# A two-layer gated cross-attention and expert kernel: earlier ranks and scatters in layer one, a later weighing step in the linear experts, phases joined by one barrier

## The reference

```
x = x + tanh(g_xattn[0]) * attention0(layernorm(x), ctx)      # 16 heads, causal
x = x + tanh(g_ffn[0])   * (experts0(h) + shared0(h))         # h = layernorm(x)
x = x + tanh(g_xattn[1]) * attention1(layernorm(x), ctx)      # 16 heads, masked by a length
x = x + tanh(g_ffn[1])   * experts1(layernorm(x))
```

## Time and profile before

| | before |
|---|---|
| median of 3 runs | 1680.35 us (1679.78 to 1683.46) |
| the profiled execution: its time, its span | 1675.68 us, 1674.0 us |
| TensorE busy, granted clock over the span | 1395.6 us, 0.927 |
| VectorE, ScalarE, GpSimd busy | 1056.6, 799.0, 729.8 us |
| layer 0 from 60 to 531 us, linear experts 535 to 748 us | |
| layer 1 from 753 to 1236 us, its experts 1244 to 1674 us | |

### The profile page before, as it was taken

The page is one execution under the profiler, slowest core; times in us unless marked ns, Lnnn a source line. Parts: engine busy times, 40 slices in busy tenths (PEclk is TensorE's granted clock), DMA queues, the critical chain, the costliest instruction groups (busy, mean ns, idle before and its releaser), DMA issues. The chain is left out here.

```text
span 1674.0 us, 39790 instructions
## 1 busy us (share of the span) xinstructions
PE 1395.6 (83%) x12001; PEld 1168.8 (70%) x12002; DVE 1056.6 (63%) x3525; ACT 799.0 (48%) x1760; POOL 729.8 (44%) x710
## 2 busy tenths in 40 slices
PE   4898998989884777746899989988629999999997
PEld 3677777767663677744565666656419999999997
DVE  3677676866765454534788888887545545555543
ACT  2454554545441555542556555565404444444443
POOL 4234443444433466555245455553323524545422
PEclk9799898999996899886899999999959999999999
DMA  5634633342314577656445534433152433343422
GB/s 119 94 91 115 177 101 111 89 116 60 97 50 130 124 122 133 103 88 109 85 111 161 119 110 121 115 88 109 44 157 41 99 63 78 88 100 89 100 38 43
DMA packets 212268, 166.92 MB, mean 100 GB/s; under 512 B 21382, under 2 KB 205736, under 8 KB 211880
## 3 DMA queue, kind: packets, MB, share of 16 engines
q1 hardware_dynamic: 178472, 125.26, 29.0%
q0 software_dynamic: 26880, 35.80, 12.4%
q10 hardware_dynamic: 6784, 4.21, 1.5%
HBM read 63.80 MB, written 50.24 MB: 68 GB/s over the span
## 5 line engine op out<-in xcount | busy, mean ns | idle before, releaser
L1896 POOL DMA_INDIRECT out_rows<-e_y,e_token x68 | 109.8, 1615 | 236.2 <-DVE e_y L1952 216.4
L1978 ACT ACTIVATE e_h<-e_h,t_up_bias 128x256 f32<-128x256 f32 x272 | 110.5, 444 | 208.0 <-PE e_h L2014 208.0
L1316 ACT ACTIVATE a_probs<-a_scores_t 128x384 f32<-128x384 f32 (+1 forms) x256 | 138.0, 544 | 118.7 <-PE a_scores_t L1683 57.8
L969 DVE TENSOR_REDUCE a_row_max<-a_scores 128x2 f32<-128x512 f32 x256 | 168.7, 677 | 19.3 <-PE a_scores L1665 19.1
L1316 ACT ACTIVATE s_w_rows<-a_scores_t 128x384 f32<-128x384 f32 (+1 forms) x256 | 138.5, 548 | 85.5 <-PE a_scores_t L1680 37.9
L807 POOL TENSOR_TENSOR a_rest<-a_qk,a_parts 128x512 f32<-128x512 f32 x64 | 72.6, 1154 | 225.2 <-ACT a_parts L1283 225.2
L797 POOL DMA_INDIRECT routed_rows_dram<-r_rows,r_slot x128 | 127.3, 994 | 91.2 <-DVE r_rows L1062 57.0
L2029 PE MATMUL e_y_bank<-e_down_hi,e_hidden_hi 128*128 128x256 f32 x544 | 157.7, 290 | 2.0 <-DVE e_hidden_lo L1925 2.0
L2014 PE MATMUL e_h<-e_xs_hi,e_up_hi 128*128 128x256 f32 x544 | 154.6, 284 | 3.9 <-DVE e_xs_lo L1917 3.8
L2187 POOL DMA_INDIRECT x_mid_dram<-l_y,l_token x76 | 118.9, 1564 | 86.7 <-ACT l_token L2281 48.2
L2029 PE MATMUL e_y_bank<-s_k_stack,e_hidden_hi 128*128 128x256 f32 x544 | 153.8, 283 | 0.0
(11 more groups left out here) (286 smaller groups left out, 4333.2 us busy)
## 6 DMA issues: line engine op xcount, KB each, us to landing
s_q_stack<-a_parts SPq DMA_DIRECT2D x384, 64.0 KB
s_k_stack<-a_parts SPq DMA_DIRECT2D x360, 64.0 KB
l_xs_rows<-routed_rows_dram SPq DMA_DIRECT2D x42, 258.0 KB
e_xs_rows<-routed_rows_dram SPq DMA_DIRECT2D x36, 258.0 KB
a_ctx_rows<-in_ctx SPq DMA_DIRECT2D x32, 256.0 KB, 3.4
t_up<-in_L_ffn_W SPq DMA_DIRECT2D x8, 1024.0 KB
t_down<-in_L_ffn_W SPq DMA_DIRECT2D x8, 1024.0 KB
x_rows<-in_x SPq DMA_DIRECT2D x16, 256.0 KB, 3.0
```

What stands on the lines that cost most here:

```text
L969: nc.vector.reduce_max(row_max[:, :, h], bank[:].rearrange("p (c t) -> p c t", c=TC), AX_X).then_inc(maxed, 1)
L1316: nc.scalar.activation(probs[h % NP][:, 0:width], scores_t[h % 2][:, 0:width], ACT.Exp).then_inc(probs_ready, 1)
L1896: pool.indirect_dma_start(out=x_acc, out_offset=bass.IndirectOffsetOnAxis(ap=token[p][:, c:c + 1], axis=0), in_=y[p][:, c, :], in_offset=N ...
L1978: nc.scalar.activation(out, h_bank[g][:, at:at + TS], act_func, bias=routed.up_bias[:, bass.ds(e * FC + fc, 1)]).then_inc(hidden_ready, 1)
```

## The change

The core of the diff, cut down:

```diff
-        DOWN_AT = 6
+        DOWN_AT = 8
+        def soon(i):
+            return soft and i.has(0)
+        def rank_at(i):
+            return 6 if soon(i) else RANK_AT
...
             pipeline(sp, step, B, FIRST, LAST, HEAD, TAIL)
-            sp.wait_ge(x_stored, (B + spares + 1) * 16)
-            sp.wait_ge(pads_sent, E * 16)
...
                 if i.has(-1):
                     route_rstd(i)
-                    if soft:
-                        bias_x(i)
                 if i.has(4):
                     rstd_of(i.at(4))
                 if i.has(-2):
                     send_rows(i)
+                if soft and i.has(-1):
+                    bias_x(i)
...
-                    if h == RANK_AT + 1 and i.has(-2):
+                    if h == rank_at(i) + 1 and i.has(-2):
                         place_rows(i)
-                    if h == 11 and i.has(-2):
+                    if h == (8 if soon(i) else 11) and i.has(-2):
                         weigh_rows(i)
-                    if h == 10 and i.has(-2):
+                    if h == (7 if soon(i) else 10) and i.has(-2):
                         copy_rows(i)
-                    if h == 11 and i.at(-2) == B - 1:
+                    if h == 15 and i.at(-2) == B - 1:
                         act.wait_ge(r_consts_ready, 1)
                         pad_regions(act, 1)
...
             def shared_down(i):
-                if not i.has(0):
-                    need(pe, counted, b + 1)
-                else:
-                    need(pe, x_updated, i.upto(-1))
+                pe.wait_ge(counted, b + 1)
...
 # expert_phase and linear_experts, at the start of each engine's stream
+            wait_all_sent(sp, keep, layer, SCATTERED)
+            sp.wait_ge(keep.pads_sent[layer], E * 16)
...
+            pool.wait_ge(keep.x_stored[layer], (tokens // P // TT + 1) * 16)
+            clear_ranges(pool, stale)
+            wait_all_sent(pool, keep, layer, SCATTERED)
...
+            nc.scalar.activation(unused[:], keep.tanh_gates[:, 0:1], act_func)
...
 # expert_phase, the first expert's weights
             if split:
-                cut_weights_hi(dve, 0, 0)
-                cut_weights_lo(dve, nc.vector, 0, 0)
+                cut_first_hi(dve)
+                cut_up_lo(nc.vector, 0, 1)
             turn_out(0, 0)
             if split:
+                dve.wait_ge(w_hi_done, 1)
+                cut_down_lo(nc.vector, 0, 1)
                 cut_weights_hi(dve, 1, 1)
...
 # linear_experts, ScalarE
-                if i.has(0):
-                    weigh(i)
+                if i.has(-1):
+                    weigh(i.at(-1), i.par(-1), i.half(-1))
...
-    clear_semaphores(nc, all_sems + held.all_sems)
+    return all_sems + held.all_sems
```

More of the change, by code:

```diff
@@ L99, in __init__ @@
         self.pads_sent = [ctx.enter_context(nc.semaphore(f"pads_sent{layer}")) for layer in range(2)]
+        self.x_stored = [ctx.enter_context(nc.semaphore(f"x_stored{layer}")) for layer in range(2)]
         self.y_sent = [[ctx.enter_context(nc.semaphore(f"y_sent{layer}{n}")) for n in range(2)] for layer in range(2)]
@@ L102, in __init__, with clear_ranges @@
         self.pad_rows = sb("pad_rows", [P, TT, ROW], F32)
+def clear_ranges(pool, sems):
+    first = 0
+    nums = sorted(s.num for s in sems)
+    for n in range(len(nums)):
+        if n + 1 == len(nums) or nums[n + 1] != nums[n] + 1:
+            pool.sem_clear(range(nums[first], nums[n] + 1))
+            first = n + 1
 def clear_semaphores(nc, ctx_sems):
@@ L109, in _, with wait_all_sent @@
         def _(pool):
-            first = 0
-            nums = sorted(s.num for s in ctx_sems)
-            for n in range(len(nums)):
-                if n + 1 == len(nums) or nums[n + 1] != nums[n] + 1:
-                    pool.sem_clear(range(nums[first], nums[n] + 1))
-                    first = n + 1
+            clear_ranges(pool, ctx_sems)
+def wait_all_sent(eng, keep, layer, count):
+    for n in range(2):
+        eng.wait_ge(keep.rows_sent[layer][n], count)
 def setup_phase(nc, keep, g_xattn, g_ffn):
@@ L235, with __init__ @@
 class ExpertWeights:
-    def __init__(self, nc, ctx, layer, D, F, ahead=None):
+    def __init__(self, nc, ctx, sem_ctx, layer, D, F, ahead=None):
         tag = f"t{layer}_"
@@ L272, in load_first, with layer_phase @@
         eng.dma_start(self.down_bias[:], row.to_broadcast((P,) + tuple(down_b.shape))).then_inc(self.bias_loaded, 16)
-def layer_phase(nc, keep, routed, stacks, layer, x_in, ctx_in, lens, weights, biases, F, up_b, gate, shared, load_experts, xs, x_acc):
+def layer_phase(nc, keep, routed, stacks, layer, x_in, ctx_in, lens, weights, biases, F, up_b, gate, shared, load_experts, xs, x_acc, sem_ctx, stale):
     B, S, D = ctx_in.shape
@@ L547, in layer_phase @@
         pads_sent = keep.pads_sent[layer]
-        x_stored = rsem("x_stored")
+        x_stored = keep.x_stored[layer]
         if soft:
@@ L1571, in project_v @@
                 if i.has(-2):
[L1572 removed]
+                    need(pe, sh_added if soft else counted, i.upto(-2))
                 elif i.has(-1):
@@ L1581, in rank @@
                 b = i.at(-2)
-                if soft and i.has(0):
-                    need(pe, sh_added, b + 1)
-                elif i.has(-1):
+                if i.has(-1):
                     need(pe, x_updated, i.upto(-1))
@@ L1723, in step @@
                             mix_group(i, 0, h // GH - 1)
+                    if h == rank_at(i) and i.has(-2):
+                        rank(i)
                     if h == GATE_AT and i.has(-2):
@@ L1733, in step @@
                         turn_xn(i)
-                    if h == RANK_AT and i.has(-2):
-                        rank(i)
                     if h == 10 and soft and i.has(-2) and not i.has(0):
@@ L1746, in _, with expert_phase @@
             pipeline(pe, step, B, FIRST, LAST, HEAD, TAIL)
-    clear_semaphores(nc, all_sems)
-def expert_phase(nc, keep, routed, held, layer, F, act_func, up_w, down_w, down_b, xs, x_acc, load_ahead=None, ahead=None, stacks=None):
+    return all_sems
+def expert_phase(nc, keep, routed, held, layer, F, act_func, up_w, down_w, down_b, xs, x_acc, load_ahead=None, ahead=None, stacks=None, sem_ctx=None, stale=()):
     D = keep.x.shape[2]
@@ L1767, in sem @@
         def sem(name):
-            s = ctx.enter_context(nc.semaphore(tag + name))
+            s = sem_ctx.enter_context(nc.semaphore(tag + name))
             all_sems.append(s)
             return s
-        own = held if held is not None else ExpertWeights(nc, ctx, layer, D, F, ahead)
+        own = held if held is not None else ExpertWeights(nc, ctx, sem_ctx, layer, D, F, ahead)
         up, down, down_bias = own.up, own.down, own.down_bias
@@ L1981, in step @@
                         round_hidden(t, g)
+            wait_all_sent(act, keep, layer, SCATTERED)
+            if split:
+                round_first_down(act)
+            nc.scalar.activation(unused[:], keep.tanh_gates[:, 0:1], act_func)
             used = used_tiles(act)
@@ L2204, in _ @@
         def _(dve):
+            wait_all_sent(dve, keep, 0, SCATTERED)
             for n in range(2):
@@ L2287, in step @@
                     bend(i)
-                if i.has(0):
-                    weigh(i)
+                if i.has(-1):
+                    weigh(i.at(-1), i.par(-1), i.half(-1))
+            wait_all_sent(act, keep, 0, SCATTERED)
+            nc.scalar.activation(unused[:], keep.tanh_gates[:, 0:1], act_func)
             used = used_tiles(act)
-            pipeline(act, step, AHEAD, FIRST, LAST, HEAD, TAIL, while_below=used)
+            pipeline(act, step, AHEAD, FIRST, LAST, HEAD + 2, TAIL, while_below=used)
+            last_used = act.value_load(routed.used_tiles[0:1, 1:2], min_val=2 * tokens // TS - 1, max_val=tiles - 1)
+            rounds = last_used // 2
+            weigh(rounds * 2 + 1, 1, rounds)
         @block.tensor
@@ L2366, in gated_flamingo @@
     with ExitStack() as ctx:
+        sems = [ctx.enter_context(ExitStack()) for phase in range(4)]
         keep = Resident(nc, ctx, tokens, D)
```

95 lines of the change are left out of this document (63 added, 32 removed).

## The result

The changed kernel takes 1712.04 us (median of 4 runs, 1702.79 to 1722.57) against 1681.23 us for the kernel before beside it: ratio 1.0184, interval 1.0118 to 1.025. It is slower, and I had forecast 1642.7.

What follows compares the result with a forecast made beforehand. TensorE was busy 1395.6 of 1674.0 us, so gains lie where it stands still or clocks lower. Terms -7.5 - 4 - 9.2 - 13 - 4 = -37.7 took 1675.68 to 1638.0, plus 4.67 to the median 1642.7; range 1620 to 1664.

Steps and rivals of the forecast that it cites:

- layer 0's loop: Layer 0's steps: shared product moves to head 8, scatters start sooner, no new wait ends last; -4 us, ends -24 and +18.
- The 0.69 us of the bend: Layer 0's loop: VectorE's bend of the shared hidden values, taken as 0.69 us, no longer stands ahead of `chosen`.
- The burst: Layer 0's four scatters: start some 7 us sooner, over heads 10 to 13; a sixth of the 24.2 us stall goes.
- Linear experts: Tile loop of the linear experts: weighing one step later lets TensorE's 4.23 us bound tiles; -13 us, bounds 0 and -20.
- The ring: Linear experts: ScalarE and VectorE wait for each other, 4.69 us per tile; weighing one step later cuts this.
- First boundary: Layer 0 to the linear experts: pads behind the bend, fewer barriers, earlier row load; -7.5 us, bounds 4.3 or 9.
- The 3 us for the pads: Layer 0's end: issuing pad DMAs after the bend brings the last store of x about 3 us earlier.
- Second boundary: Linear experts to layer 1: only the clearing and one barrier go from a 4.9 us silence; -4 us, bounds 2 and 4.9.
- Third boundary: Layer 1 to its experts: -7 for the silence, -2.2 for earlier rounding of rows; sum -9.2 us, bounds 5 and 11.
- The 2.2 us for the first cut: Layer 1's experts, first tile: cutting the down weights later lets VectorE's rounding follow the turned rows; -2.2 us.
- The rival on the slower side: Layer 0's loop: every head under the scatters waits, 5 us net per step, slower than before at 1702 us; chance 0.04.
- the grown stall: Rival in layer 0's loop: the stall under the scatters grows, +18 us instead of -4, time 1665; chance 0.10.

Runs made afterwards that it cites:

- experiment 1: The changed kernel with layer 0's loop as it was before: 1606.41 us against 1631.23 for the kernel before, ratio 0.9835.
- experiment 2: The changed kernel with only the scatters put back behind the bias of x: 1652.00 us, ratio 1.0114 to the kernel before.
- experiment 8: The changed kernel unaltered, run again on a later chip: 1649.91 us, ratio 1.0113 to the kernel before.
- experiment 9: The kernel before, unaltered, run again for a trace on a later chip: ratio 1.0005.
- experiment 4: The changed kernel with the bend of the shared hidden values at head 4 again: 1622.78 us, ratio 0.9938 to the kernel before.
- experiment 5: The changed kernel with GpSimd's third part of q and k cut to 8 columns, leaving out computation: 1617.32 us, ratio 0.9926 to the kernel before.
- 3: The changed kernel with layer 0's heads as before, but scatters early, ahead of the bias of x: 1613.80 us, ratio 0.9885 to the kernel before.
- 13: Repeat of experiment 1 (changed kernel, layer 0's loop as before) in a later job: 1603.88 us, ratio 0.9839 to the kernel before.
- 14: Repeat in a later job of the changed kernel with heads as before and scatters early: 1607.93 us, ratio 0.9855 to the kernel before.
- 16: The changed kernel with the bend at head 4 and scatters late, behind the bias of x, in a later job: 1615.18 us, ratio 0.9899 to the kernel before.
- 15: Repeat of experiment 4 (changed kernel, bend at head 4, early scatters) in a later job: 1617.67 us, ratio 0.9923 to the kernel before.
- experiment 12: Repeat of experiment 1 (changed kernel, layer 0's loop as before) in a later job: ratio 0.9871 to the kernel before.

## Why the prediction was wrong, step by step

- **The step that failed** is the sentence in the part on layer 0's loop: "VectorE's `chosen` is ready by then ... No new wait ends last, I think." I followed the rank to its input and not to its consumer. `chosen` was ready; what was late is the count, for which the diff made the shared product wait. VectorE's stream between `chosen` and the count holds two heads' maxima, the bend and the statistics, and I left out all of it. TensorE stood 2.2 us per step for the count, and worked at the lower clock behind it. The runs put this at 45 us over the loop on the later chips (experiments 1, 2, 8, 9), of which the move of the bend makes 27 to 29 (experiment 4). The term that I gave this loop was -4, with ends of -24 and +18; it came to +67.8 on the first chip.
- **The 0.69 us of the bend** was right for head 4 and wrong for head 6, where it meets GpSimd's parts: 1.39 us. I didn't look which GpSimd work stands beside the operation that moves. Experiment 5 shows that this work makes the difference, and that it is 0.7 of the 2.2 us of the wait.
- **The burst.** That it would start some 7 us sooner was about right (6 to 9). Its price can't be settled. On the first chip TensorE stood 30.5 us behind ScalarE in the new place against 24.2 in the old, and the first chip's extra loss over the later ones is 22.7 us in the loop; that the burst made this is argued from the trace only. On the later chips, four pairs of kernels that differ in the burst alone (1 and 3, 13 and 14, 2 and 8, 16 and 15) differ by 7.4, 4.1, -2.1 and 2.5 us, small beside the 30.5. What makes handoffs late on the first chip stays open.
- **Linear experts**: -13 forecast, -14.3 measured on the first chip and -12.7 on a later one (211.2 against 198.5, experiments 9 and 12). The ring and TensorE's 4.23 us were read rightly. That the later weighing makes all of it was wrong: the saved load alone makes 6.6, which I hadn't counted at all. So the closeness of the sum is in part luck.
- **First boundary**: -7.5 forecast, -5.0 measured. The 3 us for the pads came (2.9). The rest, 4.5 us for barrier and clearing, was 2.1.
- **Second boundary**: -4 forecast, with 2 as its lower bound, and -0.6 measured. The step "only the clearing and one barrier go", right as such, was priced at 4 us; the silence is GpSimd's drain of 3.90 us, and that remained. No row that I had read named what filled the silence.
- **Third boundary**: -9.2 forecast, -5.5 measured. The 2.2 us for the first cut came (8.36 - 6.09 = 2.3); the 7 us for the barrier were 3.2.
- **The rival on the slower side** ended at 1702, with a chance of 0.04. Its place, late handoffs in mid-step, is one of the two that were seen on the first chip, but the late count, which makes the whole loss on the later chips, stood in no rival. The range was said to take in the rivals up to the grown stall and ended at 1664, 1 us short of that rival's 1665.

Of the sum of -37.7 us, -33.7 was forecast for what lies outside the loop. It came to 27.0 us on the first chip (2.7 of them ahead of the loop), and experiment 1 measured 24.8 on a later one. That kernel, layer 0's loop as before with the rest of the change, is the best version: 0.9835 to 0.9871 of the kernel before in three jobs.

## What to carry to other kernels

When a wait is exchanged, follow the new semaphore to the instruction that raises it, and list everything that its engine has queued ahead of it; a value whose input is early can still be late. When a VectorE operation with two inputs in SBUF moves, look at what GpSimd reads at the new place, since both can become longer: here VectorE's took twice as long and GpSimd's a fifth more. A wait that recurs can cost more than its own length, as the granted clock behind it shows: 2.2 us of wait made steps 3.6 to 5.1 us longer. A silence at a barrier is to be named by the queue's own instructions before it is priced: the clearing that was removed took a tenth of a microsecond, and the drain that remained took four.

## What the runs showed of the hardware that was not expected

- In the kernel before, GpSimd's drain at a block's end took 3.90 us behind landed scatters and 5.29 us at the ends of the layers, and 0.04 us in blocks without DMA of its own (the clearing blocks).
- The same kernel took 1681 us on the first chip and 1630 to 1632 on four others. Of the 47.4 us between two profiled spans (1674.0 and 1626.6), 41.2 are in layer 0 (395.5 against 354.3), where ScalarE took TensorE's results under a burst of scatters after 4.7 us in the mean on the one and after 1.8 on the other.
- In experiment 8 TensorE stood still 2.2 us in mid-step, the clock fell behind it (0.50 from 326 to 330 us), and its mean from 200 to 400 us was 0.92. With standstills of 0.9 us (experiment 4) and 1.5 us (experiment 5) at the same place that mean was 0.99.
- VectorE's operation with two SBUF inputs took 1385 ns in place of 687 beside GpSimd's subtraction of the parts, a small one 745 in place of 184, and GpSimd's own 1380 in place of 1158.
